# First unit of the adjacency loaded in four half-width transfers, and TensorE started on the left half

## The chip, the cores and the metric

The kernel runs on one NeuronCore of a Trainium2 chip. The metric is the device time of one execution in microseconds (us); 1412.84 us is the median of three timed executions of the kernel before. Engines: PE is TensorE, with PEld its weight loads; DVE is VectorE, ACT is ScalarE, POOL is GpSimd, SP is SyncE, which here only issues DMA transfers.

## What is computed

Four graph layers over one adjacency matrix `adj` (4096 x 4096, float32) and features `x` (4096 x 128), each followed by a residual and a layer norm:

```python
x = _layernorm(x + _L0(x, adj, adj))   # adj @ (scale[:, None] * (adj @ (x @ weight))) + bias
x = _layernorm(x + _L1(x, adj))        # relu(inv_deg[:, None] * A_prime @ x @ W.T + b), A_prime = a*adj + (1-a) on the diagonal
x = _layernorm(x + _L2(x, adj))        # normalised adj, z, four nearest rows of z, adj again
x = _layernorm(x + _L3(x, adj))        # max([x, adj @ x] @ W.T + b, 0)
```

So six products adj @ (4096 x 128) are needed, and the row sums of adj.

## The kernel before

adj is read from memory once in float32, in 8 chunks of 512 rows (`CHUNK`), and each chunk in 8 units of 512 columns (1 MB each). SP loads the units (`load_natural`, L398 to L415) into four buffers `nat[0]` to `nat[3]`, each unit as two transfers (`b` = 0, 1) of 256 rows and all 512 columns; in SBUF a partition holds 4 rows of 512 values. After each unit of the first chunk SP also issues one part of x (`load_x0`, L382, 256 KB); part 0 comes from ACT's queue. The semaphore `nat_loaded[s]` counts 16 per transfer, so a unit is there at `NAT_LOADED` = 32. A buffer is loaded anew when its four column tiles are transposed and its row sums taken (L404 to L408).

TensorE (`transposing_chunk`, L1351) goes through the 32 column tiles `kt` of a chunk, four per unit. A tile is turned by four transposes (`turn`, L1359 to L1362), one for each `t`, the four row groups a partition holds; tile `kt` reads only the columns `b * BLOCK + j` in steps of 2, with `b = kt % 4 // 2`: tiles 0 and 1 of a unit lie in its left 256 columns, 2 and 3 in its right ones. ACT copies the turned tile to float16 (high part, `split_high`, L697), DVE forms the low part (`split_low`, L1113), and both take row sums of the natural unit in between (L710, L1125): DVE of rows t = 0 and 2, ACT of t = 1 and 3, always over all 512 columns. Four tiles behind (`LAG` = 4), TensorE multiplies a split tile into the first product of adj (`products_of`, L1321): three matmuls of 512 columns (L1341, L1343, L1345), with transposes between them. The split tiles are kept in SBUF or stored (`at_scratch`) by POOL and read again in the later passes (L1291 to L1293).

The order of the work around the start is that of the instruction streams. PE waits for `nat_loaded` when `kt % 4` is 0 (L1354 and L1355). ACT waits for it behind the copy of a unit's second tile (L703 and L704), DVE behind the low part of its first tile (L1123 and L1124). POOL loads the ten parameters once unit 2 has landed (L507 to L509); DVE uses them behind tile 15 (`setup_products`, L1117 and L1118).

Of the kernel before, what the change touches and what calls it, by code (L numbers as in the profile page):

```python
# [30 lines left out]
CHUNK = 512  # L31
TPC = CHUNK // P
PAIR = 2
NAT_LOADED = 16 * TPC // PAIR
BLOCK = PAIR * P
# [47 lines left out]
def gnn_kernel(nc, x, adj, d_list, w0, filt, bias0, alpha, w1, b1, wz, bz, w2, b2, w3, b3, out):  # L83
# [19 lines left out]
    with ExitStack() as ctx:  # L103
# [6 lines left out]
        def sem(name):  # L110
            return ctx.enter_context(nc.semaphore(name))
# [141 lines left out]
        y0_ready = sem("y0_ready")  # L253
        y0_high = sem("y0_high")
        setup_pe, setup_dve = sem("setup_pe"), sem("setup_dve")
        nat_loaded = [sem(f"nat_loaded{s}") for s in range(4)]
        rows_summed_act, rows_summed_dve = sem("rows_summed_act"), sem("rows_summed_dve")
        tr_done, high_done, low_done = sem("tr_done"), sem("high_done"), sem("low_done")
# [93 lines left out]
        def first(c):  # L352
            return isinstance(c, int) and c == 0
# [43 lines left out]
        def _(sp):  # L397
            def load_natural(c, par, m):  # L398
                for u in range(NAT_UNITS):
                    s = u % 4  # L400
                    if not (isinstance(c, int) and c == 0 and u < 4):

                        before = c * NAT_UNITS + (u - 4) + 1
                        sp.wait_ge(tr_done, before * TPC)  # L404
                        sp.nop(nofuse=True)
                        sp.wait_ge(rows_summed_dve, before * ROW_PIECES)
                        sp.nop(nofuse=True)
                        sp.wait_ge(rows_summed_act, before * ROW_PIECES)  # L408
                    for b in range(TPC // PAIR):
                        sp.dma_start(nat[s][:, b * PAIR:(b + 1) * PAIR, :],  # L410
                                     adj[bass.ds(c * CHUNK + b * BLOCK, BLOCK), u * CHUNK:(u + 1) * CHUNK]
                                     .rearrange("(p j) k -> p j k", j=PAIR)).then_inc(nat_loaded[s], 16)
                    if isinstance(c, int) and c == 0 and u + 1 < X_PARTS:
                        load_x0(sp, u + 1)
# [61 lines left out]
            for kt in range(KEPT, KT):  # L476
                u, k = divmod(kt - KEPT, UNIT)
# [184 lines left out]
        def _(act):  # L662
# [12 lines left out]
            def split_high(c, par, m):  # L675
                for kt in range(KT):
                    g = c * KT + kt
                    act.wait_ge(tr_done, g + 1)
                    if kt == 0 and c == PARKED:
                        act.wait_ge(parked_stored, 16 * PARKED_UNITS)  # L680
                    if kt < KEPT:
                        dst = kept[:, c, kt, 0, :]
                    elif is_parked(c, kt):
                        dst = parked(kt, kt + 1)[:, 0, 0, :]
                    else:
                        u = (kt - KEPT) // UNIT
                        s = (par * UPC + u) % 2
                        if (kt - KEPT) % UNIT == 0 and c * UPC + u >= 4:
                            if u == 1:
                                act.wait_ge(acc_full, c)  # L690
                            else:
                                act.wait_ge(stage_used, c * (UPC - 1) + u - 1 if u > 1 else c * (UPC - 1))
                        for part, (k0, k1) in enumerate(STORES):
                            if (kt - KEPT) % UNIT == k0 and c * UPC + u >= 4:
                                act.wait_ge(stage_stored[s][part], 16 * ((c * UPC + u) // 2 - 1))
                        dst = stage[s][:, (kt - KEPT) % UNIT, 0, :]
                    nc.scalar.activation(dst, pt[kt % 4][:, :], ACT.Copy, scale=A_SCALE).then_inc(high_done, 1)  # L697
                    if first(c) and kt % XT_PART == 0 and kt > 0:
                        y0_high_part(kt // XT_PART)
                    if kt % 2 == 1:  # L700
                        u, t = divmod(kt, TPC)
                        n = c * NAT_UNITS * ROW_PIECES + u * ROW_PIECES + t // 2
                        if t == 1:  # L703
                            act.wait_ge(nat_loaded[u % 4], NAT_LOADED * (c * 2 + u // 4 + 1))  # L704
                        if kt == 1 and not (isinstance(c, int) and c < 2):
                            act.wait_ge(rows_closed, c - 1)
                        if not (first(c) and u == 0):
                            act.wait_ge(rows_summed_act, n - 1)
                        discard = (xin, xout)[t // 2][:, :, :].rearrange("p t f -> p (t f)").bitcast(BF16)
                        nc.scalar.activation(discard[:, 0:CHUNK], nat[u % 4][:, t, :], ACT.Copy,  # L710
                                             accum_out=rs_part[par][:, u, t:t + 1]).then_inc(rows_summed_act, 1)
                    if kt == 7 and not first(c):
                        act_epilogue(act, 0, c - 1, 1 - par)
                    if kt == KT - 1 and not (isinstance(c, int) and c < 2):
                        act.wait_ge(part_full, c - 1)
                        if not isinstance(c, int) or c > 2:
                            act.wait_ge(part_stored, 16 * (c - 2))
                        nc.scalar.activation(xT[:, :], pxT[:, :], ACT.Copy, scale=1.0 / (A_SCALE * Y_SCALE[0])
                                             ).then_inc(part_ready, 1)
                        act.wait_ge(part_ready, c - 1)  # L720
                        act.dma_start(part_dram[bass.ds(c, 1), :, :].rearrange("c p n -> (c p) n"), xT[:, :]
                                      ).then_inc(part_stored, 16)
# [146 lines left out]
            for h in range(2):  # L869
                half = slice(h * TPC // 2, (h + 1) * TPC // 2)  # L870
# [11 lines left out]
        def _(dve):  # L882
# [218 lines left out]
            def split_low(c, par, m):  # L1101
                for kt in range(KT):
                    g = c * KT + kt
                    dve.wait_ge(high_done, g + 1)
                    if kt < KEPT:
                        hi = kept[:, bass.ds(c, 1), kt, 0, :].rearrange("p c n -> p (c n)")
                        lo = kept[:, bass.ds(c, 1), kt, 1, :].rearrange("p c n -> p (c n)")
                    elif is_parked(c, kt):
                        hi, lo = (parked(kt, kt + 1)[:, 0, h, :] for h in range(2))
                    else:  # L1110
                        s = (par * UPC + (kt - KEPT) // UNIT) % 2
                        hi, lo = (stage[s][:, (kt - KEPT) % UNIT, h, :] for h in range(2))
                    nc.vector.scalar_tensor_tensor(lo, pt[kt % 4][:, :], A_SCALE, hi, ALU.mult,  # L1113
                                                   ALU.subtract).then_inc(low_done, 1)
                    if first(c) and kt % XT_PART == 1 and kt > XT_PART:
                        y0_part(kt // XT_PART)
                    if first(c) and kt == 15:  # L1117
                        setup_products()  # L1118
                    if first(c) and kt == 24:
                        setup_copies()  # L1120
                    if kt % 2 == 0:
                        u, t = divmod(kt, TPC)
                        if t == 0:  # L1123
                            dve.wait_ge(nat_loaded[u % 4], NAT_LOADED * (c * 2 + u // 4 + 1))  # L1124
                        nc.vector.tensor_reduce(rs_part[par][:, u, t:t + 1], nat[u % 4][:, t, :],  # L1125
                                                AXX, ALU.add).then_inc(rows_summed_dve, 1)
                    if kt == 14 and not first(c):
                        scale_projected(c - 1)
                    if kt == 15 and not first(c):
                        counted(0, c - 1, lambda: split_projected(c - 1))  # L1130
                dve.wait_ge(rows_summed_dve, (c + 1) * NAT_UNITS * ROW_PIECES)
                dve.wait_ge(rows_summed_act, (c + 1) * NAT_UNITS * ROW_PIECES)
                nc.vector.tensor_reduce(rs[:, bass.ds(c * TPC, TPC)], rs_part[par][:, :, :].rearrange("p u t -> p t u"),
                                        AXX, ALU.add).then_inc(rows_closed, 1)
# [161 lines left out]
        def _(pe):  # L1296
# [54 lines left out]
            def transposing_chunk(c, par, m):  # L1351
                for kt in range(KT):
                    u = kt // TPC
                    if kt % TPC == 0:  # L1354
                        pe.wait_ge(nat_loaded[u % 4], NAT_LOADED * (c * 2 + u // 4 + 1))  # L1355
                    if not (first(c) and kt < 4):
                        pe.wait_ge(low_done, c * KT + kt - 3)
# [326 lines left out]
```

## Time and profile before

| | us |
|---|---|
| timed executions | 1411.88, 1412.84, 1417.01 (median 1412.84) |
| the profiled execution | 1415.97 |
| its span, first to last instruction | 1414.3 |
| PE busy | 1385.4 |
| DVE, ACT, POOL busy | 842.8, 457.6, 239.5 |

The profile is of one execution. Times in its rows count from the start of the span. The chain that ended last is followed back from the last instruction, at each step to what released it or to the instruction before it on its engine; it says which engine's time the span consists of. PE's busy time holds its work at either of the clock's two levels, so a busy PE can be a slow one.

### The profile page before, as it was taken

To read this page: it belongs to the slowest core of one execution; us is meant where nothing else is said; L and a number is where in the kernel's file an instruction comes from. 1 tells how busy PE (TensorE), PEld (TensorE's weight loads), DVE (VectorE), ACT (ScalarE), POOL (GpSimd) and SP (SyncE) were. 2 spreads that over 40 slices of the span, in tenths; PEclk is the share of its full clock that TensorE was granted. 3 is DMA by queue.
4 is the path that set the end of the run, shared out by engine and by line. 5 is a ranking of instruction groups with operands and counts; after the bars stand their busy time and mean duration, and the time that the engine had idled before them with its cause. 6 is when DMAs were issued, how large, how long until landed. Compare 5 with 4: busy or idle time off the path is not lost.

```text
span 1414.3 us, 19936 instructions
## 1 busy us (share of the span) xinstructions
PE 1385.4 (98%) x7369; PEld 795.8 (56%) x7369; DVE 842.8 (60%) x1306; ACT 457.6 (32%) x967; POOL 239.5 (17%) x362
## 2 busy tenths in 40 slices
PE   7999999999999999999999999999999999999998
PEld 6888887777544445544444545444444444444467
DVE  6877776666323423434323259999999946655144
ACT  6766665555300000000000126655555410000011
POOL 1111111110100100000000000111111167777000
PEclk9999999999999999999999999999999999999999
DMA  9999989887999879997787803303444699999973
GB/s 326 383 381 390 361 325 348 338 301 269 340 390 354 346 301 390 411 359 296 299 320 273 324 19 98 104 16 119 134 135 134 220 390 405 403 372 400 386 252 116
DMA packets 111410, 407.53 MB, mean 288 GB/s; under 512 B 11664, under 2 KB 28048, under 8 KB 89568
## 3 DMA queue, kind: packets, MB, share of 16 engines
q1 hardware_dynamic: 79520, 316.43, 60.0%
q0 software_dynamic: 19440, 73.71, 13.3%
q10 hardware_dynamic: 12368, 16.26, 3.2%
q8 instruction: 55, 0.90, 0.2%
q14 instruction: 27, 0.22, 0.0%
HBM read 339.77 MB, written 66.58 MB: 287 GB/s over the span
## 4 chain that ended last, share of the span: by engine, by line
PE 75%; DVE 17%; DMA 5%; ACT 1%; issue 1%; SPq 0%; DVEq 0%
PE acc L1291 10%; PE acc L1293 10%; PE acc L1292 10%; DVE hT L1176 8%; PE pt L1361 6%; PE pt L1291 5%; PE pt L1293 5%; PE pt L1292 5%; DVE wT L1177 4%; DMA region<-in_adj 4%; DVE wz_sb L1177 3%; PE acc L1341 3%; PE acc L1345 3%; PE acc L1343 3%; PE pnat L1258 2%; PE pxT L1332 1%
## 5 line engine op out<-in xcount | busy, mean ns | idle before, releaser
L1361 PE MATMUL pt<-ident,region 128*128 128x128 f32 x1024 | 242.6, 278 | 14.4 <-DMA region<-in_adj 14.2
L1361 PEld LDWEIGHTS pt<-ident,region 128*128 128x128 f32 x1024 | 200.4, 196 | 40.1 <-issue 9.0
L1291 PE MATMUL acc<-region,yop 128*128 128x512 f16 (+1 forms) x581 | 217.8, 375 | 0.4 <-DMA region<-at_scratch 0.4
L1293 PE MATMUL acc<-region,yop 128*128 128x512 f16 (+1 forms) x581 | 217.5, 374 | 0.0
L1292 PE MATMUL acc<-region,yop 128*128 128x512 f16 (+1 forms) x581 | 217.5, 374 | 0.0
L1113 DVE SCALAR_TENSOR_TENSOR region<-pt,region 128x512 f16<-128x512 f32 x190 | 129.2, 687 | 71.7 <-ACT region L697 71.4
L747 ACT ACTIVATE region<-pt 128x512 f32<-128x512 f32 x256 | 133.0, 603 | 112.0 <-PE pt L1457 46.5
L697 ACT ACTIVATE region<-pt 128x512 f16<-128x512 f32 x190 | 112.2, 595 | 99.6 <-PE pt L1361 91.6
L1176 DVE MAX8 hT<-region 128x8 f32<-128x4096 f32 x31 | 136.6, 4406 | 1.3 <-ACT region L747 1.3
L1450 PE MATMUL pt<-yop 128*128 128x512 f16 x256 | 98.0, 383 | 5.8 <-ACT region L747 4.2
L654 ACT ACTIVATE std<-mv,eps_ln 128x4 f32<-128x4 f32 x31 | 9.2, 297 | 284.6 <-DVE mv L920 284.6
L1451 PE MATMUL pt<-yop 128*128 128x512 f16 x256 | 97.0, 379 | 0.0
L1452 PE MATMUL pt<-yop 128*128 128x512 f16 x256 | 97.0, 379 | 0.0
L1291 PE MATMUL pt<-region,yop 128*128 128x512 f16 x250 | 94.8, 379 | 1.5 <-DMA region<-at_scratch 1.4
L1292 PE MATMUL pt<-region,yop 128*128 128x512 f16 x250 | 94.8, 379 | 0.0
L1293 PE MATMUL pt<-region,yop 128*128 128x512 f16 x250 | 94.8, 379 | 0.0
L1291 PEld LDWEIGHTS acc<-region,yop 128*128 128x128 f16 x581 | 56.8, 98 | 66.4 <-issue 5.7
L1293 PEld LDWEIGHTS acc<-region,yop 128*128 128x128 f16 x581 | 56.8, 98 | 65.9
L518 POOL DMA_DIRECT2D at_scratch<-region x76 | 40.4, 532 | 307.1 <-DVE region L1113 307.1
L1292 PEld LDWEIGHTS acc<-region,yop 128*128 128x128 f16 x581 | 56.9, 98 | 60.0
L1125 DVE TENSOR_REDUCE rs_part<-region 128x1 f32<-128x512 f32 x128 | 86.5, 676 | 0.0
L1341 PE MATMUL acc<-region,yop 128*128 128x512 f16 x190 | 72.0, 379 | 0.7 <-DVE yop L1070 0.7
(261 smaller groups left out, 2301.9 us busy)
## 6 DMA issues: line engine op xcount, KB each, us to landing
region<-at_scratch SPq DMA_DIRECT2D x163, 1280.0 KB, 8.2
region<-in_adj SPq DMA_DIRECT2D x128, 512.0 KB, 8.0
at_scratch<-region POOLq DMA_DIRECT2D x38, 768.0 KB, 7.0
at_scratch<-region POOLq DMA_DIRECT2D x38, 512.0 KB, 7.1
region<-at_scratch SPq DMA_DIRECT2D x76, 256.0 KB, 2.7
x_scratch<-xout ACTq DMA_DIRECT2D x16, 256.0 KB, 11.1
region<-at_scratch ACTq DMA_DIRECT2D x3, 1280.0 KB, 9.7
gath_all<-x_scratch POOLq DMA_DIRECT2D x12, 256.0 KB, 5.2
```

The costliest lines, as they stand in the source:

```text
L697: nc.scalar.activation(dst, pt[kt % 4][:, :], ACT.Copy, scale=A_SCALE).then_inc(high_done, 1)
L747: nc.scalar.activation(near[i % 2][:, j * CHUNK:(j + 1) * CHUNK], near_bank(i, j)[:, :], ACT.Copy).then_inc(near_copied, 1)
L1113: nc.vector.scalar_tensor_tensor(lo, pt[kt % 4][:, :], A_SCALE, hi, ALU.mult, ALU.subtract).then_inc(low_done, 1)
L1176: step(nc.vector.max(top8[:, i, :], near[i % 2]))
L1177: nc.vector.max_index(idx8(i), top8[:, i, :], near[i % 2]).then_inc(near_used, 1)
L1291: nc.tensor.matmul(into, y[:, 0, kt, :], high, start=(kt == first_tile), stop=False)
L1292: nc.tensor.matmul(into, y[:, 0, kt, :], low, start=False, stop=False)
L1293: return nc.tensor.matmul(into, y[:, 1, kt, :], high, start=False, stop=(kt == last_tile))
L1341: nc.tensor.matmul(acc[par][:, :], yh, hi, start=(kt == 0), stop=False)
L1361: ins = nc.tensor.transpose(pt[kt % 4][:, t * P:(t + 1) * P], nat[u % 4][:, t, b * BLOCK + j:(b + 1) * BLOCK:PAIR], ident[:, :])
L1450: nc.tensor.matmul(into, zh, zT[:, 0, cols], start=True, stop=False)
L1451: nc.tensor.matmul(into, zh, zT[:, 1, cols], start=False, stop=False)
```

## The change

The first unit of the first chunk is loaded by four transfers in place of two: the left 256 columns of both row blocks, counted by a new semaphore `first_half`, and then the right 256 columns of both, counted by `nat_loaded[0]`, which so still reaches 32. Each of these transfers moves 256 KB in row pieces of 1 KB, where each of the two before moves 512 KB in pieces of 2 KB. All other units are loaded as before. PE waits for `first_half` ahead of tile 0 and for `nat_loaded[0]` ahead of tile 2 of that unit. ACT and DVE wait for both ahead of their first row sum.

```diff
+        first_half = sem("first_half")
@@ load_natural (SP)
-                    for b in range(TPC // PAIR):
+                    if first(c) and u == 0:
+                        for half, loaded in enumerate((first_half, nat_loaded[0])):
+                            for b in range(TPC // PAIR):
+                                sp.dma_start(nat[0][:, b * PAIR:(b + 1) * PAIR, half * CHUNK // 2:(half + 1) * CHUNK // 2],
+                                             adj[b * BLOCK:(b + 1) * BLOCK, half * CHUNK // 2:(half + 1) * CHUNK // 2]
+                                             .rearrange("(p j) k -> p j k", j=PAIR)).then_inc(loaded, 16)
+                    for b in range(0 if not (first(c) and u == 0) else TPC // PAIR, TPC // PAIR):
@@ split_high (ACT)
+                        if first(c) and kt == 1:
+                            act.wait_ge(first_half, NAT_LOADED)
                         if t == 1:
                             act.wait_ge(nat_loaded[u % 4], NAT_LOADED * (c * 2 + u // 4 + 1))
@@ split_low (DVE)
+                        if first(c) and kt == 0:
+                            dve.wait_ge(first_half, NAT_LOADED)
                         if t == 0:
                             dve.wait_ge(nat_loaded[u % 4], NAT_LOADED * (c * 2 + u // 4 + 1))
@@ transposing_chunk (PE)
-                    if kt % TPC == 0:
+                    if first(c) and kt == 0:
+                        pe.wait_ge(first_half, NAT_LOADED)
+                    if (kt == TPC // 2) if first(c) and u == 0 else kt % TPC == 0:
                         pe.wait_ge(nat_loaded[u % 4], NAT_LOADED * (c * 2 + u // 4 + 1))
```

## Rows read from the trace of the kernel before

**Rows 1.** The page: PE's busy time, the chain by engine, two groups of products.
```profile
PE 1385.4 (98%) x7369; PEld 795.8 (56%) x7369; DVE 842.8 (60%) x1306; ACT 457.6 (32%) x967; POOL 239.5 (17%) x362
...
PE 75%; DVE 17%; DMA 5%; ACT 1%; issue 1%; SPq 0%; DVEq 0%
...
L1291 PE MATMUL acc<-region,yop 128*128 128x512 f16 (+1 forms) x581 | 217.8, 375 | 0.4 <-DMA region<-at_scratch 0.4
...
L1291 PE MATMUL pt<-region,yop 128*128 128x512 f16 x250 | 94.8, 379 | 1.5 <-DMA region<-at_scratch 1.4
```

**Rows 2.** The chain in order of time, its first pieces: start, duration, what.
```profile
0.87 0.69 SPq L410
1.61 6.83 DMA region<-in_adj
8.44 0.14 issue
8.57 3.87 PE pt L1361 x17
12.44 0.22 PE acc L1341
```

**Rows 3.** Issues: duration min/median/max, starts, to landing; units 0, 1, 2; x 0, 1.
```profile
L410 SPq DMA_DIRECT2D region<-in_adj x2: 591/640/688, 0.9 to 1.6; - x2
DMA to landing us min/median/max: 4.2/5.5/6.8
...
L410 SPq DMA_DIRECT2D region<-in_adj x2: 551/582/612, 2.9 to 3.5; - x2
DMA to landing us min/median/max: 7.4/7.8/8.3
...
L410 SPq DMA_DIRECT2D region<-in_adj x2: 912/1037/1162, 5.3 to 6.5; - x2
DMA to landing us min/median/max: 8.4/8.6/8.7
...
L382 ACTq DMA_DIRECT2D yop<-in_x x1: 443/443/443, 0.9 to 0.9; - x1
...
DMA to landing us min/median/max: 2.9/2.9/2.9
...
L382 SPq DMA_DIRECT2D yop<-in_x x1: 594/594/594, 2.3 to 2.3; - x1
```

**Rows 4.** Stretches: length, five engines, granted clock, DMA share, GB/s.
```profile
2.00:3.00 1.00, 0.00 (x0) 0.00 (x0) 0.00 (x0) 0.83 (x2) 0.00 (x0) 1.00 0.84 240
3.00:4.00 1.00, 0.00 (x0) 0.00 (x0) 0.00 (x0) 0.25 (x1) 0.00 (x0) 1.00 0.99 365
...
5.00:8.57 3.57, 0.00 (x0) 0.03 (x1) 0.11 (x1) 0.00 (x0) 0.00 (x0) 1.00 0.93 289
8.57:11.81 3.24, 3.24 (x15) 3.24 (x16) 1.48 (x3) 1.85 (x5) 0.00 (x0) 1.00 1.05 387
...
25.00:26.00 1.00, 1.00 (x8) 0.87 (x7) 1.00 (x3) 0.51 (x2) 0.00 (x0) 1.00 0.74 191
```

**Rows 5.** The timeline of 0 to 14 us: DVE's first low part, SP's unit 4.
```profile
10.33 0.69 DVE L1113 SCALAR_TENSOR_TENSOR kept<-pt,kept 128x512 f16<-128x512 f32 x1 [5.23 <-ACT kept L697]
...
13.65 0.54 SPq L410 DMA_DIRECT2D region<-in_adj  x1
```

**Rows 6.** Transposes of 9 to 12 and of 13 to 20 us: ns min/median/max.
```profile
L1361 PE MATMUL pt<-ident,region x16: 417/417/457, 8.6 to 11.8; 128*128 128x128 f32 x16
...
L1361 PE MATMUL pt<-ident,region x27: 271/273/284, 12.8 to 19.9; 128*128 128x128 f32 x27
```

**Rows 7.** The parameters: POOL's last issue and its landing, DVE's use, PE's wait.
```profile
20.50 0.54 POOL L509 DMA_DIRECT2D alpha_c<-in_L_gnn_alpha x1
...
DMA to landing us min/median/max: 5.7/6.0/6.4
...
27.12 0.41 DVE L1076 TENSOR_TENSOR hT<-hT 48x256 f32<-48x256 f32 x1
...
30.89 0.38 PE L1341 MATMUL acc<-kept,yop 128*128 128x512 f16 x1 [0.80 <-DVE yop L1070]
```

**Rows 8.** PE's waits from 13 to 420 us, and from 160 to 166.
```profile
PE pt L1361 <- DMA region<-in_adj: 5.7, 4, 3.0
...
PE pt L1361 <- DMA region<-in_adj: 1.2, 1, 1.2
```

**Rows 9.** Stretches around two waits (columns as in 4); transposes and products of 265:268.
```profile
161.00:165.00 4.00, 2.62 (x15) 1.91 (x14) 3.11 (x6) 4.00 (x10) 0.27 (x2) 1.00 1.03 415
165.00:168.00 3.00, 3.00 (x20) 2.74 (x20) 2.38 (x6) 2.02 (x6) 0.82 (x2) 1.00 1.04 413
...
261.80:264.85 3.05, 0.02 (x1) 0.00 (x0) 2.30 (x4) 1.23 (x4) 0.00 (x0) 1.00 1.04 417
264.85:268.30 3.45, 3.44 (x10) 1.84 (x11) 0.00 (x0) 0.00 (x0) 0.00 (x0) 0.51 1.03 410
...
L1361 PE MATMUL pt<-ident,region x3: 421/421/487, 264.9 to 267.5; 128*128 128x128 f32 x3
...
L1331 PE MATMUL pxT<-kept,yop 128*128 128x512 f16 x1 | 0.6, 634 | 0.0
```

**Rows 10.** The chain at two later loads, and stretches at or before them.
```profile
74.30 0.58 SPq L410
75.06 11.55 DMA region<-in_adj
...
250.14 0.55 SPq L410
250.87 13.95 DMA region<-in_adj
...
75.00:80.00 5.00, 5.00 (x34) 4.56 (x33) 3.60 (x6) 3.21 (x8) 1.06 (x2) 1.00 1.03 415
...
225.00:230.00 5.00, 5.00 (x34) 3.85 (x33) 1.97 (x3) 2.19 (x5) 1.59 (x3) 1.00 0.71 253
```

## The prediction

> **What bounds the kernel now.** The page comes first: TensorE (PE) is busy for 98% of the span, and the chain that ended last is 75% PE, 17% DVE and 5% DMA [rows 1]. An edit at the front can give back only time in which PE stands still, and only as long as nothing later takes it back. The chain in order of time gives the size of what is aimed at: the first unit's second transfer lands at 8.44 us, PE's first transpose starts at 8.57, 17 transposes follow, and the first product is at 12.24 to 12.44 [rows 2]. PE is idle for 8.57 us. The landing times then say when each unit is there: a row gives the first and last start of the issues and the time from issue to landing. Unit 0 lands at 0.87 + 4.2 = 5.1 and about 1.6 + 6.8 = 8.4; unit 1's second transfer at about 3.5 + 8.3 = 11.8; unit 2's at 6.5 + 8.7 = 15.2 [rows 3]. Then how fast the DMA engines move, by stretch [rows 4], what the engines do between 8 and 14 us [rows 5], at which level PE's clock stands [rows 6], where DVE waits for parameters [rows 7], and the later waits of PE [rows 8 to 10].
>
> The reader is to see one thing above all. Unit 0 takes 16 transposes. The group of 17 ends at 8.57 + 3.87 = 12.44 and one lasts 417 ns [rows 2, 6], so the 17th starts at 12.02, and they follow each other at (12.02 - 8.57) / 16 = 0.216 us. The 17th is the first of unit 1. Unit 1 is there at 11.8. PE now comes to unit 1 only about 0.2 us after it has landed. An earlier start of 3 us turns into a wait for unit 1.
>
> **The change part by part.**
>
> *Issues on SP.* Two transfers of 512 KB become four of 256 KB. Each takes SP 0.59 to 0.69 us [rows 3]; a 256 KB one of x takes 0.59 too [rows 3]. So two more issues, 2 x 0.6 = 1.2 to 1.3 us. They stand ahead of x's part 1 and of unit 1: unit 1's issues move from 2.9 and 3.5 to 4.1 and 4.7. Behind them on SP stand all further loads. Cover: unit 1 takes 7.4 to 8.3 us from issue to landing, while a 256 KB transfer into a nearly empty queue took 2.9 [rows 3], so some 4.5 us of that is queueing, and I cost the issue at nothing. Without the cover it would cost the 1.3 us. The later issues of this first round are stretched to 0.9 to 1.2 us (unit 2) [rows 3], as an issuer held back by full queues would show.
>
> *The left half.* 512 KB, the same bytes as the first transfer of now, behind the same 256 KB of x from ACT's queue. That transfer lands at 5.1. The second left transfer is issued 0.69 us after the first, but its data queue behind the first's anyway. I take 5.1 to 5.5 for the later of the two, PE's start 0.14 behind it: 5.2 to 5.7, or 2.9 to 3.4 us earlier than now. The other bound is no head start at all: the second transfer of unit 0 lands 3.3 us after the first although it was issued 0.7 after it, so a single transfer can be held up.
>
> *Smaller runs.* Each row piece is 1 KB instead of 2 KB, for 1 MB. From 2 to 3 us mostly x's 1 KB pieces moved: 240 GB/s at a share of 0.84, or 286 per full share; from 3 to 4 mostly 2 KB pieces: 365 at 0.99, or 369 [rows 4]. One MB (1.05 million bytes) is 3.67 us by the one and 2.84 by the other: at most 0.8 us more, at least nothing (the first stretch also has the queues' start in it). I take the middle, 0.4. From 2 us on the DMA engines are busy at 0.92 to 1.05 until past 20 us, with the first real gap at 25 to 26 us, 0.74 [rows 4]. What is added to the queue ahead of unit 1 therefore delays unit 1: 11.8 + 0.4 = 12.2.
>
> *PE.* Transposes of column tiles 0 and 1 need only the left half: 8 x 0.216 = 1.7 us, from about 5.3 to 7.0. Then the new wait for the right half, which comes at 6.5 (its share of the bytes) to 8.4 (now's landing of unit 0). Tiles 2 and 3: 1.7 us, done at 8.7 to 10.1. Then the old wait for unit 1, until 12.2 + 0.14 = 12.3, against 12.02 now: +0.3 us. Behind that wait stand the first products too, since product kt 0 is issued behind the first transpose of kt 4. This is where the head start goes, whatever its size.
>
> *ACT and DVE.* ACT waits for the right half behind the copy of tile 1, DVE behind the low part of tile 0; queued behind those waits are the row sums and the splits of tiles 1 to 3. Now the split of tile 0 is done at 10.33 + 0.69 = 11.02 [rows 5] and PE needs it at 12.24; with transposes ended at 10.1 at the latest, the splits of tiles 0 to 3 are ready before 12.3. Nobody waits: nothing. Slot 0 comes free earlier too, so unit 4 is asked for at about 11.5 instead of 13.65 [rows 5]; the queue is full then, and PE has no wait for unit 4 now (after 13 us there are only four for adj, all later, below). Nothing.
>
> *The clock.* The transposes of unit 0 last 417 ns, those from 13 us on 273 [rows 6]; after a later wait three last 421 ns in a stretch with a granted clock of 0.51 [rows 9]. So PE works at its low level (1.2 GHz) from 8.57 until about 12.3 and at 2.4 GHz after it, though the clock column says 1.00 for this early stretch. It rose after 3.7 us of work without a pause, just when the products began; transposes lose nothing by it that was needed before unit 1. After the change PE works 1.7 us, pauses up to 1.4, works 1.7, and pauses 2 to 3.6. At 261.80 to 264.85 PE stood still for 3.05 us, and the next 3.45 us ran at 0.51 [rows 9]; a wait of 1.2 us shortly before 165 us was not followed by it (the clock is 1.00 from 161 to 168) [rows 8, 9]. So I expect the low level at 12.3, for about as long as either row has it, 3.45 to 3.7 us. There lie products, which at the low level take 634 ns each [rows 9] instead of the 374 to 379 they take over the whole run [rows 1]: 3.45 x 0.49 = 1.7 us lost. The bounds are 0 (risen in time and not fallen) and, with a rise that comes once more as late, 3.4.
>
> The Trainium skill bears on this, in "TensorE: Matmul & The Clock Gate", section "HAM oscillation — how this bites in real kernels": bursts of matmuls shorter than the waits for the next load keep the array at its half rate. It speaks against this change, which makes two short bursts out of one. By that rule the sum has the 1.7, without it the 0.3 alone; the rows at 265 us agree with it.
>
> *What is left at the end.* Splits, setup and products follow PE: +2.0 us at 16 us. At 27.12 DVE starts the parameter products, and the last parameter lands at 20.5 + 6.4 = 26.9 [rows 7]; a gain could not pass here by more than 0.2 us, a loss passes. PE waits four more times for adj, 5.7 us in all, the longest 3.0 [rows 8]. The first load of those is asked for at 74.30, by a chain through PE and ACT, and takes 11.55 in queues whose share is 1.03 [rows 10]; the last at 250.14, behind a stretch with a share of 0.71 [rows 10]. Where the queues were full the loss is swallowed by the wait, where they had gaps it is passed on. I take a quarter swallowed, 0.5; the bounds are all and nothing. Sum: 0.3 + 1.7 - 0.5 = +1.5 us.
>
> **The rivals.**
>
> 1. *The head start is lost, the clock costs nothing.* As above without the 1.7: 0.3 us, between -0.3 (unit 1 where it is, no added wait) and +0.9. For: the later work before 12.3 may have raised the clock, since the two bursts nearly join if the right half comes by 7 us. Against: the pause behind them. 1412.8 + 0.3 = 1413.1.
> 2. *The head start is kept,* -3.4 us, 1409.4. It needs unit 1 at 8.8 us instead of 11.8; that would be units 0 and 1 and two parts of x, 2.62 million bytes, in 6.8 us, 386 GB/s from 2 us on without a dip. 5.0 to 8.57 shows 289 [rows 4]. It also has to pass the 26.9 of the parameters.
> 3. *The change doesn't do what it says:* the left half comes no earlier than about 8 us because a transfer is held up as the second one now is. PE starts as now and unit 1 is 0.4 later: 1413.2.
> 4. *Slower beyond rival 1: another long wait like that at 262 us.* The shifted loads meet the stores differently and one of the three shorter waits (5.7 - 3.0 = 2.7 us in all, one of them 1.2, so the other two some 0.7 each [rows 8]) grows to 3 us and the clock falls behind it: 3.05 - 0.7 + 1.7 = 4.0 us; with the start's 2.0, 1418.8. It decides where a wait becomes as long as that one of 3.05 us. Against: the shift is 2 us at most, and loads shift with their consumers. To leave the 0.5% band it needs two such, 1412.8 + 2.0 + 8.0 = 1422.8.
>
> **How the numbers follow.** The profiled execution took 1415.97 us (span 1414.3), 3.1 above the median of 1412.84; the three timed ones are 1411.88 to 1417.01, so runs differ by more than every term here. My sum on its own base is 1415.97 + 1.5 = 1417.5; on the median it is 1412.84 + 1.5 = 1414.3, and that I give. Chances: forecast 43%, rival 1 33%, rival 2 4%, rival 3 9%, rival 4 11% (of it 3% beyond the band). About 0.5%, or 7.1 us, can be told from no change. A median can sit anywhere in 1411.9 to 1417.0 by the runs alone; shifted by -0.3 to +1.5 and with the edges cut to 8 in 10, the range is 1411.3 to 1417.3. It leaves out rival 2 and most of rival 4. Faster by over 0.5% needs twice the whole head start: 1%. Slower by over 0.5%: 3%. Within: 96%.
>
> **What would show it.** After the change: PE's first transpose at 5.2 to 5.7; a wait for adj ahead of tile 2 of up to 1.4 us; a new wait of 2 to 3.6 us for adj that ends at 12.0 to 12.6, with 16 transposes before it; mean durations of the transposes behind it 417 (forecast) or 273 (rival 1) until about 16 us; PE's wait of 0.80 us for DVE ahead of 30.89 [rows 7] still there, 0.3 to 2 us later. The forecast is wrong if unit 1 lands before 11 us (rival 2), if the first transpose is after 8 (rival 3), or if the waits for adj after 80 us add up to over 8 us (rival 4).

## The result

| | kernel before | changed kernel |
|---|---|---|
| median of 21 executions each | 1414.77 us | 1416.88 us |
| lowest, highest | 1410.74, 1418.37 | 1411.76, 1423.75 |
| the profiled execution (its span) | 1415.97 (1414.3) | 1413.48 (1411.8) |

The changed kernel is slower: the ratio is 1.0022, 95% interval 1.0012 to 1.0032, or 3.1 us (1.7 to 4.5). That is within the 0.5% band, and twice the 1.5 us of the forecast; the two medians alone are 2.1 us apart. Two later measurements of the same kernel gave 1.0017 (1.0005 to 1.0029) and 1.0008 (0.9994 to 1.0021). The mean of the three ratios is 1.0016, or 2.2 us.

The profiled pair seems to say the opposite, 2.5 us less. So the first reading must be where the two traces part. The page of the changed kernel, lines of [rows 1]; L1302 is L1291 of before:

```profile
PE 1385.8 (98%) x7369; PEld 795.5 (56%) x7369; DVE 843.1 (60%) x1306; ACT 457.6 (32%) x967; POOL 238.7 (17%) x362
...
PE 75%; DVE 17%; DMA 6%; ACT 1%; issue 1%; SPq 0%; DVEq 0%; ACTq 0%
...
L1302 PE MATMUL acc<-region,yop 128*128 128x512 f16 (+1 forms) x581 | 217.7, 375 | 0.1
```

Nothing is to be seen at that level. PE's timeline of the first 45 us, only the groups behind a wait, in the changed kernel (start, duration, what, then idle time and its releaser):

```profile
6.45 3.66 PE L1374 MATMUL pt<-ident,region 128*128 128x128 f32 x16 [6.45 <-DMA region<-in_adj]
11.94 0.38 PE L1374 MATMUL pt<-ident,region 128*128 128x128 f32 x1 [1.84 <-DMA region<-in_adj]
32.39 0.38 PE L1352 MATMUL acc<-kept,yop 128*128 128x512 f16 x1 [0.80 <-DVE yop L1079]
42.84 0.38 PE L1352 MATMUL acc<-region,yop 128*128 128x512 f16 x1 [0.67 <-DVE yop L1079]
```

PE starts 2.1 us earlier than in [rows 2], finishes the 16 transposes of unit 0 in one stretch at 10.10, without the forecast wait for the right half, and waits 1.84 us for unit 1. The product behind DVE's 0.80 us wait, at 30.89 in [rows 7], is at 32.39: 1.50 us later. This product is the milestone of all that follows ("the 31 us product"). Stretches of the same profile (columns as in [rows 4]) show what came between:

```profile
2.00:12.00 10.00, 3.72 (x17) 3.35 (x17) 4.41 (x7) 4.96 (x11) 0.00 (x0) 1.00 0.93 295
10.10:11.94 1.84, 0.00 (x1) 0.00 (x1) 1.78 (x3) 1.23 (x4) 0.00 (x0) 1.00 1.05 376
13.39:16.80 3.41, 3.41 (x13) 2.19 (x12) 2.18 (x4) 2.27 (x5) 1.15 (x2) 0.50 1.06 380
16.80:20.00 3.20, 3.20 (x22) 2.85 (x21) 2.28 (x4) 2.32 (x6) 3.20 (x7) 1.00 1.07 382
```

From 13.39 to 16.80 the granted clock is 0.50, its low level of 1.2 GHz, in the middle of products: 3.41 x 0.49 = 1.7 us by the working of the prediction. And the DMA engines moved 295 GB/s from 2 to 12 us, where before they moved 329:

```profile
2.00:12.00 10.00, 3.43 (x16) 3.46 (x17) 2.36 (x4) 3.50 (x8) 0.00 (x0) 1.00 0.97 329
```

Why is this execution shorter at the end all the same? The wait of 3.0 us for adj near 262 us, with its fall of the clock [rows 9], did not come. PE's waits for adj, first before, then after, from 260 to 268 us:

```profile
PE pt L1361 <- DMA region<-in_adj: 3.0, 1, 3.0
...
PE pt L1374 <- DMA region<-in_adj: 0.4, 1, 0.4
```

In the further profiles it was 2.9 us in the second one of the kernel before, 2.4 and 0.5 in those of the changed one, and anything from none to 2.8 in the variants below. It differs by 2 us between executions of one kernel, so one pair of profiles can't be read against it; whether the change makes it rarer, two profiles against three can't tell. What the change does for certain has to be read in the first 45 us.

### The profile page after: what moved, and what is told of

Same layout as the page of the kernel before. It is cut to its first block, busy times and chain, and to the rows that moved or that the text cites. A ratio compares the mean times of both kernels' runs of the same rounds, so it can differ in the third digit from the quotient of the medians.

```text
span 1411.8 us, 19940 instructions
## 1 busy us (share of the span) xinstructions
PE 1385.8 (98%) x7369; PEld 795.5 (56%) x7369; DVE 843.1 (60%) x1306; ACT 457.6 (32%) x967; POOL 238.7 (17%) x362
## 3 DMA queue, kind: packets, MB, share of 16 engines
q0 software_dynamic: 19440, 73.71, 13.3%
## 4 chain that ended last, share of the span: by engine, by line
PE 75%; DVE 17%; DMA 6%; ACT 1%; issue 1%; SPq 0%; DVEq 0%; ACTq 0%
PE acc L1302 10%; PE acc L1304 10%; PE acc L1303 10%; DVE hT L1187 8%; PE pt L1374 6%; PE pt L1302 5%; PE pt L1304 5%; PE pt L1303 5%; DVE wT L1188 4%; DMA region<-in_adj 4%; DVE wz_sb L1188 4%; PE acc L1352 3%; PE acc L1354 3%; PE acc L1356 3%; PE pnat L1269 2%; PE pxT L1343 1%
## 5 line engine op out<-in xcount | busy, mean ns | idle before, releaser
L1302 PE MATMUL acc<-region,yop 128*128 128x512 f16 (+1 forms) x581 | 217.7, 375 | 0.1
L1302 PE MATMUL pt<-region,yop 128*128 128x512 f16 x250 | 94.8, 379 | 1.5 <-DMA region<-at_scratch 1.4
L1302 PEld LDWEIGHTS acc<-region,yop 128*128 128x128 f16 x581 | 56.8, 98 | 66.2 <-issue 5.6
```

The source lines that it names most:

```text
L1302: nc.tensor.matmul(into, y[:, 0, kt, :], high, start=(kt == first_tile), stop=False)
```

## The experiments

Fifteen runs beside the first pair; three of them are the two kernels once more, and with the variants there are twelve different kernels. In the table, unit 1 is when its second transfer landed; "clock high" is from when the clock record shows the high level to the end of the first 30 us (in brackets: high from, fell at); the last column compares timed executions with the kernel before on the same chip. All times in us.

| kernel | PE starts unit 0 | GB/s, 2 to 12 | unit 1 | clock high | 31 us product | ratio (95%) |
|---|---|---|---|---|---|---|
| before | 8.57 | 329 | 11.8 | 12.3 | 30.89 | |
| before_again | 8.52 | 334 | 11.9 | 11.7 | 32.22 (DVE waits for a parameter) | 1.0000 (0.9988 to 1.0012) |
| before_warm | 8.04 | 354 | 11.4 | 6.2 | 30.56 | 1.0010 (1.0000 to 1.0021) |
| after | 6.45 | 295 | 11.9 | 16.8 (10.0, 13.4) | 32.39 | 1.0022 (1.0012 to 1.0032) |
| after_again | 6.23 | 298 | 12.7 | 16.4 (9.6, 13.0) | 33.22 | 1.0017 (1.0005 to 1.0029) |
| after_third | 7.05 | 307 | 12.2 | 15.0 | 32.29 | 1.0008 (0.9994 to 1.0021) |
| late_start | 7.90 | 303 | 12.6 | 17.0 | 33.51 | 1.0012 (1.0001 to 1.0024) |
| fill_pause | 6.32 | 309 | 13.0 | 16.7 (9.9, 13.3) | 33.54 | 1.0007 (0.9994 to 1.0020) |
| fill_more | 6.22 | 300 | 12.3 | 11.4 | 31.71 | 1.0001 (0.9992 to 1.0011) |
| after_warm | 6.4 | 298 | 12.4 | 7.0 | 31.31 | 1.0007 (0.9993 to 1.0021) |
| long_pieces | 8.70 | 290 | 11.9 | 14.8 | 32.10 | 1.0008 (0.9995 to 1.0022) |
| right_on_act | 7.31 | 353 | 10.9 | 10.2 | 29.75 | 0.9995 (0.9985 to 1.0006) |
| right_on_act_2 | 6.77 | 347 | 11.1 | 15.2 | 31.84 | 1.0008 (0.9999 to 1.0017) |
| act_warm | 7.75 | 330 | 11.4 | 5.1 | 30.26 | 1.0018 (1.0005 to 1.0031) |
| block_on_act | 7.11 | 364 | 10.1 | 10.0 | 29.43 | 0.9989 (0.9978 to 1.0000) |
| block_on_act_2 | 8.10 | 355 | 10.7 | 13.9 | 31.37 | 0.9988 (0.9975 to 1.0001) |
| two_on_act | 7.08 | 358 | 10.3 | 6.4 | 29.22 | 0.9992 (0.9978 to 1.0007) |

An interval is 0.09 to 0.15% wide to either side, 1.3 to 2 us; the timed column tells the changed kernel from block_on_act, and little in between. The terms of 0.3 to 1.7 us are told apart by the profiles. The expectations speak of PE's 200th matmul instead of the 31 us product; it comes at about 43 us in the kernel before, and between the two all kernels but before_again keep their distance to it within 0.05 us.

**The two kernels again.** No edit.

> The kernel before once more, unchanged, timed against itself: the ratio should be 1.000 within its interval, and its second profile shows what differs between two executions of one kernel. Transfer theory (the two further issues and the 1 KB pieces delay unit 1) expects unit 1's second transfer within 0.4 us of the 11.8 of before, and PE at its 200th matmul within 0.6 us of 43.0; if unit 1 lands at 12.5 or later here too, the delay seen with four transfers is only scatter.

Unit 1 at 11.9, where 12.5 would have made the delay with four transfers mere scatter. But the first profile of the changed kernel has 11.9 too, so the delay shows only over several profiles. The 31 us product is 1.3 late all the same, by a wait that the first profile did not have. DVE's row:

```profile
28.45 0.42 DVE L1076 TENSOR_TENSOR hT<-hT 48x256 f32<-48x256 f32 x1 [1.29 <-DMA alpha_c<-in_L_gnn_alpha]
```

The parameters landed 1.3 us later than in [rows 7], and nothing covered it; the clock then fell too (0.50 from 32.20 to 35.50), which put the 200th matmul 2.7 us behind, outside what was expected. Two executions of one kernel differ by as much as the change costs.

> The changed kernel once more, unchanged, for a second profile and timed beside the others on one chip. Clock theory (the products behind the pause before unit 1 run at TensorE's low level): transposes of 417 to 421 ns or products of 634 ns for 3 to 7 us somewhere between 12 and 20 us, and 1.5 to 3.4 us more than the kernel before by then. Transfer theory (four transfers with 1 KB pieces hold up the loads behind them): unit 1 lands 0.4 to 1.3 us later than the 11.8 of before, the clock is high from 12.3 us on. Later-waits theory: by 80 us the two kernels are level, and the difference comes with PE's four later waits for adj (5.7 us in the profile of before). Time: 1 to 4 us over the kernel before by all three.

> The changed kernel a third time. Start theory (the whole loss is there at 43 us: unit 1's delay and 1.6 us of the clock): the clock falls once more between 12 and 17 us, PE at its 200th matmul 1.4 to 2.7 us behind the kernel before, and the ratio 1.001 to 1.002. If a further part of the loss came behind 43 us: PE at its 1500th matmul over 0.5 us further behind than at the 200th, in all three profiles.

Both keep PE waiting for unit 1 with 16 transposes done, 2.95 and 1.53 us, and both have products at the low level. Of after_again:

```profile
12.77 0.39 PE L1374 MATMUL pt<-ident,region 128*128 128x128 f32 x1 [2.95 <-DMA region<-in_adj]
...
13.02:16.44 3.42, 3.42 (x13) 2.10 (x12) 0.70 (x2) 1.12 (x2) 0.00 (x0) 0.50 1.07 384
```

In after_third the clock was not yet high when unit 1 came and rose at 15.0. So in three profiles of three some products ran at the low level, for 2.8 to 3.4 us. From the 200th to the 1500th matmul (256 us) the three moved by +0.4, 0.0 and -1.6 us against the kernel before: no further loss from 43 to 256 us that all share, so the later-waits theory finds no support. Nor do the profiles carry the loss further: at the 1701st matmul, 295 us in the kernel before, the three are at -2.4, +0.1 and -4.4 us against it and before_again at +2.6, by the waits near 262 us above all. Five profiles can't show how 1.4 to 2.35 us at 43 us become the loss in the timed executions.

**late_start.** PE waits for both halves before tile 0.

```diff
-                    if (kt == TPC // 2) if first(c) and u == 0 else kt % TPC == 0:
+                    if kt % TPC == 0:
```

> The four transfers stay, but PE waits for both halves of unit 0 ahead of tile 0, so its 16 transposes run in one stretch. Clock theory: PE starts at about 7.9 us, works 3.4 us, waits at most 0.6 us for unit 1, and the clock rises at about the products as before; the time is that of the kernel before within 0.5 us, some 1.5 to 3 us under the changed kernel. Transfer theory: the time is the changed kernel's, 2 to 3 us over the kernel before. Later-waits theory: anywhere between, with the difference behind 80 us.

A miss for the clock theory as I had put it. Without an early start the loss is all there in the profile, 33.51. Unit 1 lands at 12.6, which is the transfers' part, and the clock rises only at 17.0 although PE worked from 7.90 to 11.56 in one stretch. The early start of PE is not what costs; a pause in front of unit 1 comes from unit 1's delay too.

**fill_pause and fill_more.** 10 and 22 transposes of the identity into bank `pxT`, which nobody reads, between tile 3 and the wait for unit 1 of the changed kernel.

```diff
+                    if first(c) and kt in (0, TPC):
+                        idle_turns(0 if kt == 0 else 22)     # fill_pause: 10
```

> The changed kernel with 10 more transposes of the identity into a free bank between tile 3 and the wait for unit 1, which nobody reads: 1.1 us of work at the high level, 2.1 at the low one, inside the pause of 1.84 us. Clock theory: the clock does not fall behind the pause, the products from 12 us on take 379 ns each, and 1 to 1.7 us of the loss is gone. Transfer theory and later-waits theory: no change from the changed kernel.

> The changed kernel with 22 transposes of the identity between tile 3 and the wait for unit 1 and none at the start: 2.4 us of work at the high level, so less than 1 us of the pause is left (10 of them left 1.96 us and the clock still fell). Clock theory: the clock stays high, no products of 634 ns between 12 and 20 us, PE at its own 200th matmul 0.2 to 1.2 us behind the kernel before (that is unit 1's delay alone), where the changed kernel has 1.5 and 2.3. If filling the pause does nothing: 1.5 or more again.

With 10, unit 1 came late (13.0), 1.96 us of pause were left, and the clock fell as in the changed kernel: the expectation of the clock theory was missed, and the run says no more than that this was too little. With 22 no wait is left and no product is slow. PE's rows of fill_more, only groups behind a wait, and its stretch:

```profile
6.22 3.78 PE L1380 MATMUL pt<-ident,region 128*128 128x128 f32 x16 [6.22 <-DMA region<-in_adj]
31.71 0.38 PE L1352 MATMUL acc<-kept,yop 128*128 128x512 f16 x1 [0.80 <-DVE yop L1079]
...
12.00:20.00 8.00, 8.00 (x56) 7.34 (x55) 4.95 (x9) 5.24 (x12) 4.02 (x8) 1.00 1.06 384
```

56 matmuls touch 12 to 20 us, 11 of them idle ones, against 35 in after_again. The 31 us product is 0.82 us late instead of 1.40 to 2.33. Unit 1 was 0.5 late, and the 22 transposes were too many: they ran on to 12.98, where unit 1 had landed at 12.3, so a good part of the 0.82 is their own.

The clock's share can be taken out of all profiles. Take the start of PE's first transpose of unit 1, 12.02 us in the kernel before and 11.94, 12.77 and 12.24 in the three profiles of the changed one. How late it is, taken from how late the 31 us product is, leaves 1.6, 1.6 and 1.2 us. Five more profiles have products at the low level before 18 us (late_start, fill_pause, long_pieces, right_on_act_2, block_on_act_2) and leave 1.0 to 2.0. The seven others, with no slow product there, leave -0.1 to +0.3, fill_more -0.1 among them. before_again is left out for its wait for a parameter. So the clock's part comes and goes with the low level. Part of it can be in a kernel without a split too: block_on_act_2 has 1.0.

**after_warm and before_warm.** The same idle work in the pause and also ahead of tile 0 (20 and 16 in the changed kernel, 32 and 12 in the kernel before).

> The changed kernel with 20 transposes of the identity into a free bank while unit 0 is loaded and 16 more between tile 3 and the wait for unit 1. Clock theory: no stretch at the low level between 12 and 20 us, so PE at its 200th matmul of the kernel's own is later than before only by unit 1's delay, 0.1 to 1.2 us, where the changed kernel's two profiles have 1.5 and 2.3. If the loss is all from the transfers: 1.5 to 2.3 here too.

> The kernel before with 32 transposes of the identity into a free bank from 1.8 us on, while unit 0 is loaded, and 12 between tile 3 and the wait for unit 1. Clock theory: the transposes of unit 0 take 273 ns each and end by about 10.5 us, products start at 12.0 (unit 1's landing) and none of them is slow; 0.2 to 1 us under the kernel before on the mean, since its clock rises late only in some executions. If the start's clock is worth nothing: the time of the kernel before, within 0.3 us; if unit 1's landing did not bind, up to 1.9 us under it.

In the profiles both do what the clock theory says: 0.42 late with unit 1 0.7 late, and 0.33 early. The timed executions show neither: 1.0007 for after_warm can't be told from 1.0016 or from 1, and before_warm, at 1.0010, has no sign of the mean gain expected.

**long_pieces.** late_start with each of the four transfers as 64 partitions of full rows, so in pieces of 2 KB.

```diff
-sp.dma_start(nat[0][:, b * PAIR:(b + 1) * PAIR, half * CHUNK // 2:(half + 1) * CHUNK // 2],
+sp.dma_start(nat[0][half * P // 2:(half + 1) * P // 2, b * PAIR:(b + 1) * PAIR, :],
```

> Unit 0 in four transfers of 256 KB as in the changed kernel, but each of 64 partitions with the full 512 columns, so in row pieces of 2 KB; PE starts when all four are there. If it is the two further issues on SP that delay unit 1 (issued 1.3 us later), it lands at 12.6 to 13.0 as with late_start. If it is the 1 KB pieces, at 11.6 to 11.9 as before. Half of each: 12.1 to 12.4.

Unit 1 at 11.9, as before, though the issues are as many and as late as with 1 KB pieces. But the rate from 2 to 12 us is the lowest of all, 290, at a DMA share of 1.02: on 64 partitions busy engines moved less, so more than the piece is changed. It is one profile, and 11.9 is also the lowest of the seven with 1 KB pieces. It speaks for the piece, weakly.

**right_on_act.** The changed kernel with the two right transfers issued by ACT behind x's part 0.

```diff
             load_x0(act, 0)
+            for b in range(TPC // PAIR):
+                act.dma_start(nat[0][:, b * PAIR:(b + 1) * PAIR, CHUNK // 2:CHUNK], ...).then_inc(nat_loaded[0], 16)
```

> The changed kernel with the two right transfers issued from ACT's queue behind x's part 0, so that SP issues as early as before: unit 1 at 2.9 and 3.5 us. Issue theory: unit 1 lands at 11.5 to 11.9, the pause before it is shorter by 1 us, and PE at its 200th matmul is 1 us earlier than in the changed kernel. Piece theory: unit 1 still at 12.6. Clock theory by itself: the clock still falls behind the pause unless the pause is under 1.2 us.

> right_on_act once more: unit 1 at 10.8 to 11.2 if that is no scatter, PE's first transpose at about 7.3, PE at its 200th matmul about 1.1 us ahead of the kernel before; time 0 to 2 us under the kernel before.

Pieces of 1 KB as in the changed kernel, and unit 1 is 0.7 to 0.9 us earlier than before the change, at 353 and 347 GB/s. So 1 KB pieces don't delay unit 1 as long as it is issued as early as before, at 2.9 and 3.5 us, where the changed kernel has 4.2 and 4.8. What is left is that the transfers follow each other from one queue, 0.6 us for each on SP. PE's rows of the first:

```profile
7.31 3.33 PE L1378 MATMUL pt<-ident,region 128*128 128x128 f32 x16 [7.31 <-DMA region<-in_adj]
10.91 0.39 PE L1378 MATMUL pt<-ident,region 128*128 128x128 f32 x1 [0.26 <-DMA region<-in_adj]
29.75 0.38 PE L1356 MATMUL acc<-kept,yop 128*128 128x512 f16 x1 [0.80 <-DVE yop L1083]
```

Here the 31 us product is 1.14 us ahead. In the second profile it is 0.95 behind, against the expectation, with unit 1 nearly as early: the clock rose at 15.2 instead of 10.2. Its timed executions, at 1.0008, show no gain either.

**act_warm.** right_on_act with 26 and 10 idle transposes.

> right_on_act with 26 transposes of the identity while unit 0 is loaded and 10 between tile 3 and the wait for unit 1. Clock theory: no stretch at the low level before 30 us in any case, products from 11.0 us on, PE at its own 200th matmul 0.9 to 1.3 us ahead of the kernel before; time 0.5 to 2.5 us under it. If warmth is worth nothing here: the same as right_on_act.

0.63 ahead at the 31 us product, with unit 1 at 11.4 (the rate was 330), less than expected; and 1.0018 in the timed executions, slower than the kernel before. Its profile loses 3.5 us between 43 and 256 us; PE's waits for adj from 140 us on add up to 3.9 us there, 1.2 in the kernel before. Whether the timed executions have that too, one profile can't say.

**block_on_act.** The kernel before, with the second transfer of unit 0 issued by ACT. Nothing is split.

```diff
-                    for b in range(TPC // PAIR):
+                    for b in range(1 if first(c) and u == 0 else TPC // PAIR):
@@
             load_x0(act, 0)
+            act.dma_start(nat[0][:, PAIR:2 * PAIR, :],
+                          adj[BLOCK:2 * BLOCK, 0:CHUNK].rearrange("(p j) k -> p j k", j=PAIR)).then_inc(nat_loaded[0], 16)
```

> The kernel before (two transfers of 512 KB, 2 KB pieces, PE starts when both are there) with the second one issued from ACT's queue. Issue theory (what counts is how many bytes per issue of one queue stand ready early): 340 to 355 GB/s from 2 to 12 us as with right_on_act, unit 1 lands at 10.8 to 11.3, PE at its 200th matmul 0.5 to 1.1 us ahead of the kernel before, although nothing is split. If the gain of right_on_act came from the halves: unit 1 at 11.4 to 11.9 as before.

> block_on_act once more: unit 1 at 10.0 to 10.6 us, PE at its 200th matmul 1.0 to 1.6 us ahead of the kernel before; ratio 0.998 to 1.000. If the first result was scatter: unit 1 at 11.4 or later, ratio 1.000 to 1.001.

```profile
7.11 3.45 PE L1363 MATMUL pt<-ident,region 128*128 128x128 f32 x17 [7.11 <-DMA region<-in_adj]
...
2.00:12.00 10.00, 4.89 (x27) 4.78 (x28) 3.75 (x6) 5.61 (x12) 0.00 (x0) 1.00 1.02 364
```

Unit 1 at 10.1 and 10.7, and 0.9989 and 0.9988 in two measurements: both intervals end at about 1.000. It is the best version found, 1.6 us under the kernel before by the middle of the intervals. In the second profile the milestone missed its expectation, 0.5 behind instead of 1.0 to 1.6 ahead, as the clock rose at 13.9. Unit 1 is issued at 2.2 and 2.8 here, 0.7 us ahead of right_on_act, and lands 0.7 us ahead of it (means of two and three profiles, with act_warm). So far, long_pieces apart, an earlier issue of unit 1 has meant an earlier landing.

**two_on_act.** The same with unit 1's second transfer on ACT too, and 22 and 6 idle transposes.

> block_on_act with unit 1's second transfer on ACT's queue too, and with 22 transposes of the identity ahead of tile 0 and 6 behind tile 3, so that neither issues nor the clock hold PE. If issues still bound the start: unit 1 at 9.0 to 9.6 us, products from 9.8, PE at its 200th matmul 1.8 to 2.5 us ahead of the kernel before. If the transfers are by now limited by the DMA engines (364 GB/s from 2 to 12 us in block_on_act): unit 1 at 10.0 to 10.3, 1.4 to 1.9 us ahead.

Unit 1 at 10.3, no earlier than with one transfer moved, and a rate of 358 at a share of 1.00: the second of the two expected cases, the DMA engines as the limit. The lead of 1.67 us is there, and at 84 us it goes:

```profile
PE pt L1371 <- DMA region<-in_adj: 4.2, 1, 4.2
...
88.50:91.80 3.30, 3.30 (x10) 1.71 (x11) 0.00 (x0) 0.00 (x0) 0.00 (x0) 0.51 1.03 403
```

A wait for adj of 4.2 us and the low clock behind it; from 43 to 140 us the profile loses 4.7 us. This is the mechanism of rival 4, here behind a lead. It was in one profile of seventeen at this place.

## Why the prediction was wrong

The direction, the band and the mechanism were right: PE's head start turned into a wait for unit 1, and the clock at its low level in the products made a loss of it. The size was wrong, 1.5 for 3.1 (1.7 to 4.5). Up to 43 us the sum was +2.0, and the three profiles of the changed kernel have 1.5, 2.3 and 1.4, mean 1.8. The step that failed is the last one, the 0.5 us that the later waits were to swallow: in its place the time has 3.1 - 1.8 = 1.3 us more. Where that comes from stays open. The cover of the issues on SP was mis-sized too, by 0.3. By its own steps:

- *The left half:* 5.1 to 5.5 forecast. PE started at 6.45, 6.23 and 7.05, 1.5 to 2.3 us earlier instead of 2.9 to 3.4. The two left transfers are not one of the same size: in the first profile they landed at 4.6 and 6.3. It cost nothing, since the head start was lost anyway. The right half was there in time, so the two bursts of the forecast were one.
- *Issues on SP at nothing, cover 4.5 us of queueing, and smaller runs 0.4:* mis-sized, and wrong in its reason. Seven profiles with four transfers from SP in 1 KB pieces have unit 1 at 11.9 to 13.0, mean 12.4; three with two transfers have 11.4 to 11.9, mean 11.7. That is 0.7 to 0.8 us for a forecast of 0.4. The changed kernel's own three profiles, at 11.9, 12.7 and 12.2, have 0.4 against 11.8 and 11.9, so there the forecast came out. Unit 1 was issued 1.3 us later and took 7.1 to 7.9 us to land instead of 8.3: the queue covered 0.4 to 1.2 of the 1.3, not all. That from 2 us on the DMA engines were busy at 0.92 to 1.05 was misread: [rows 4] has 0.84 from 2 to 3 us and 289 GB/s from 5 to 8.57, so the cover was thinner than taken even in the kernel before. With four transfers from SP the share from 2 to 12 us is 0.93 to 0.95, with two 0.96 to 1.01; that is the smaller part of the lost rate. The rest is fewer bytes from engines that were busy, 314 to 327 GB/s per full share instead of 339 to 350, and no run shows why. An estimate from the issues, 262 kB in 0.6 us or 437 GB/s, lies above the 387 of [rows 4]: there is little reserve over what the engines move, no more is shown.
- *The clock, 1.7 us:* right in size and place. The three profiles have 3.4, 3.4 and 2.8 us at the low level in the products, and lost 1.6, 1.6 and 1.2 us by it. The history was different: twice it rose before 10 us and fell behind the pause, 1.84 and 2.95 us long, and once it rose only at 15.0; a wait of 1.2 us had not been followed by a fall [rows 8, 9]. But it is not free in a kernel without a split either. "It rose after 3.7 us of work" was one execution; with work in one stretch it took 3.1 us in before_again, 2.8 and 5.8 in the two of block_on_act and 6.1 in long_pieces. That both profiles of the kernel before escaped may be luck, and the mean cost of the clock there is not known.
- *Four later waits, a quarter swallowed, -0.5:* the step that failed. The timed loss is larger than the one at 43 us and not smaller. Between 43 and 256 us no common part was given back (+0.4, 0.0, -1.6), and the scatter there is larger than the term. With 0 there and 0.75 less the 0.2 of slack for the delay, the sum by its own steps is 0.55 + 1.6 = 2.2 us, inside the measured interval; that it is also the mean of the three ratios is no proof.
- *No gain passes 26.9 us, where the parameters land:* wrong. right_on_act and block_on_act passed with 1.1 and 1.5 us. POOL asks for the parameters when unit 2 has landed (L507), so they come earlier with it: the last is asked for at 19.6 and 19.1 us there instead of 20.5. The risk that I named on the other side is real: before_again waited 1.29 us there.
- *The base:* 1412.84 was the median of three executions; that of 21 is 1414.77, so 1.9 of the 2.6 us between 1414.3 and 1416.88 were the base. That 1416.88 lies in the range owes much to its width.
- *Rival 1* (no clock cost) holds where PE was kept at work, fill_more and after_warm. *Rival 2:* the start itself can be 1 to 1.5 us earlier, but by the queues and not by the halves. *Rival 3* did not come. *Rival 4* was seen once, in two_on_act.

What is settled: in the first 43 us the changed kernel is 1.4 to 2.35 us behind, and this is unit 1's delay plus the clock, shown in the profiles by the low level that comes and goes with the clock's part, and by fill_more and after_warm, which took it away. That the remaining 1.3 us to the 3.1 is scatter is argued, not shown; the intervals allow it. In the timed executions the cause is borne out by fill_more alone, 1.0001 (0.9992 to 1.0011) against 1.0022 (1.0012 to 1.0032). Whether piece size or the count of issues makes the delay stays open: right_on_act speaks against the piece alone, and long_pieces, with one profile, against the count alone.

The Trainium skill's section "HAM oscillation — how this bites in real kernels" ("TensorE: Matmul & The Clock Gate") describes what the changed kernel showed in its small way, bursts with load waits between them and a clock at its low level; the trace agrees in part, with 3.41 us at 0.50, but behind a burst of 3.65 us that was longer than its wait of 1.84 us. The Trainium skill's page "DMA: Bandwidth & Descriptors", section "Rules for kernel authors", says that spreading transfers over issuing engines gives no bandwidth and only saves issue time. Here unit 1, issued earlier, landed earlier, at 10.1 to 11.4 us instead of 11.4 to 11.9 in the kernel before and before_warm. The rate from 2 to 12 us is less clear: 330 to 364 GB/s with a second queue, 329, 334 and 354 with two transfers from SP alone. two_on_act showed the end of it.

## What to carry to other kernels

Before you let an engine start on a part of its first load, look when the second load lands: the head start is worth only the slack there, here 0.2 us. Don't pay for it with more issues from one queue at the very start; a second queue for some of the first transfers is the better try. Without any split unit 1 came 1.0 to 1.7 us earlier here, and the time was 1.6 us less by the middle of two intervals that both just reach 1.000. And count a pause that you open in TensorE's work as its length plus what the clock may take behind it.

## What was not expected of the hardware

- The DMA engines moved more when two queues asked: 353, 347 and 330 GB/s from 2 to 12 us with four transfers on SP and ACT, 295 to 309 with the same four on SP.
- The clock's rise is scattered: with the kernel's transposes in one stretch it came 2.8 to 6.1 us behind their start, and in late_start, with a pause of 1.12 us after 3.66 us of work, 9.1 us behind it.
- A single long wait near 262 us, 3.0 and 2.9 us in the two profiles of the kernel before and 0.4, 2.4 and 0.5 in those of the changed one, moves an execution by up to 4.7 us with the fall of the clock behind it (3.0 + 1.7), more than any effect studied here. The fall is not certain: of the seven profiles with a wait of 2.3 us or more there, four have it. One pair of profiles would have given the wrong sign.
